# Vision tower with routed experts: patch matmuls on 128 filled rows, 21 pixels a group instead of 28, the rest moved by VectorE

## The reference

```python
patches = X.reshape(B, C, 8, 28, 8, 28).transpose(0, 2, 4, 1, 3, 5).reshape(B, 64, C * 28 * 28)
tokens = einsum('bpi,hi->bph', patches, W) + b            # 2352 inputs to 128 outputs
tokens = concatenate([cls, tokens], axis=1) * pos_embed
h = tokens
h = h + attention(layernorm(h), W_c)      # scores, softmax over a window of 64, sigmoid(concat @ W_c)
h = h + moe_ffn(layernorm(h), ...)        # norm, router, top 2 of 16 experts, shared expert, feed-forward
```

## Time and profile before

| | |
|---|---|
| median of three runs | 1130.94 us |
| the profiled execution | 1132.04 us, its span 1130.3 us |
| mean granted TensorE clock | 0.952 |
| TensorE busy | 1009.2 us, 89% |
| VectorE busy | 552.6 us, 49% |
| ScalarE busy | 640.3 us, 57% |
| GpSimd busy | 382.3 us, 34% |
| patch matmuls (line 1261) | 428.3 us, 896 records |
| pair copies (line 541) | 252.0 us, 224 of 1161 ns |

### The profile page before, as it was taken

The page is one execution under the profiler, slowest core; times in us unless marked ns, Lnnn a source line. Parts: engine busy times, 40 slices in busy tenths (PEclk is TensorE's granted clock), DMA queues, the critical chain, the costliest instruction groups (busy, mean ns, idle before and its releaser), DMA issues.

```text
span 1130.3 us, 20773 instructions
## 1 busy us (share of the span) xinstructions
PE 1009.2 (89%) x4911; PEld 665.4 (59%) x4911; DVE 552.6 (49%) x2019; ACT 640.3 (57%) x1056; POOL 382.3 (34%) x399
## 2 busy tenths in 40 slices
PE   3899999999999999999524899999999859898986
PEld 2344454555554454555314899999999635554554
DVE  3034544445445434445443666666666355555543
ACT  2566676666666776666213465556655426555554
POOL 0001222333333222333352122222222476666661
PEclk9899999999999999999656999999999979999999
DMA  9965566666656666661128688888888312222321
GB/s 228 236 172 148 169 180 182 183 183 204 186 178 178 173 180 181 188 189 37 38 86 269 201 249 249 247 247 249 248 244 237 102 53 80 79 80 80 87 60 35
DMA packets 208005, 186.36 MB, mean 165 GB/s; under 512 B 16909, under 2 KB 182378, under 8 KB 207722
## 3 DMA queue, kind: packets, MB, share of 16 engines
q1 hardware_dynamic: 192400, 156.82, 48.9%
q0 software_dynamic: 12256, 27.81, 7.4%
q10 hardware_dynamic: 3322, 1.44, 0.5%
HBM read 150.15 MB, written 35.85 MB: 165 GB/s over the span
## 4 chain that ended last, share of the span: by engine, by line
PE 71%; POOL 12%; issue 8%; SPq 3%; DVE 3%; DMA 2%; ACT 0%; DVEq 0%; POOLq 0%; ACTq 0%
PE bank L1261 36%; PE bank L1399 12%; PE bank L1388 10%; POOL region L799 9%; PE bank L1266 3%; SPq L376 2%; POOL rstd L733 2%; PE bank L1377 2%; PE bank L1274 1%; PE bank L1282 1%; PE bank L1296 1%; PE bank L1339 1%; PE bank L1341 1%; DVE region L881 1%; DMA region<-in_x 1%
## 5 line engine op out<-in xcount | busy, mean ns | idle before, releaser
L1261 PE MATMUL bank<-xf,wp 128*128 128x512 f32 x896 | 428.3, 618 | 7.6 <-ACT xf L541 7.6
L541 ACT ACTIVATE xf<-region 84x1024 f32<-84x1024 f32 x224 | 252.0, 1161 | 50.8 <-DMA region<-in_x 30.6
L1261 PEld LDWEIGHTS bank<-xf,wp 128*128 128x128 f32 x896 | 160.4, 190 | 182.2 <-issue 168.6
L647 ACT ACTIVATE region<-bank,cols 128x256 f32<-128x256 f32 x320 | 135.0, 477 | 119.1 <-PE bank L1388 119.1
L733 POOL TENSOR_TENSOR rstd<-var,neghalf 128x4 f32<-128x4 f32 (+2 forms) x51 | 63.1, 1237 | 390.4 <-DVE var L890 299.0
L1399 PE MATMUL bank<-region 128*128 128x128 f32 x1280 | 156.4, 276 | 0.0
L1399 PEld LDWEIGHTS bank<-region 128*128 128x128 f32 x1280 | 150.7, 193 | 0.0
L799 POOL DMA_INDIRECT region<-y_rows,gidx x130 | 126.4, 972 | 68.2 <-issue 36.3
L749 POOL DMA_INDIRECT z_rows<-z,posg x130 | 128.2, 986 | 37.5 <-issue 37.5
L1388 PE MATMUL bank<-parts 128*128 128x256 f32 x960 | 136.6, 292 | 3.8 <-DVE parts L1093 2.8
L778 POOL DMA_DIRECT2D y_rows<-region x80 | 58.1, 727 | 233.7 <-DVE region L1077 224.7
(11 more groups left out here) (169 smaller groups left out, 1123.8 us busy)
## 6 DMA issues: line engine op xcount, KB each, us to landing
region<-in_x SPq DMA_DIRECT2D x384, 196.0 KB
region<-in_L_ffn_ew SPq DMA_DIRECT2D x160, 256.0 KB, 3.4
region<-z_rows SPq DMA_DIRECT2D x80, 128.0 KB, 2.8
y_rows<-region POOLq DMA_DIRECT2D x80, 128.0 KB, 3.1
out<-region SPq DMA_DIRECT2D x65, 64.0 KB
ht_dram<-hT SPq DMA_DIRECT2D x16, 256.0 KB, 3.4
r_dram<-rr SPq DMA_DIRECT2D x16, 256.0 KB, 3.6
region<-ht_dram SPq DMA_DIRECT2D x16, 256.0 KB, 5.4
```

Source lines behind the costliest of these rows:

```text
L541: act.activation(pair_of(i)[0:KROWS], pixels(k, i), ACT.Copy).then_inc(xact_ready, 1)
L647: act.activation(ehT[n % 2][:, c], bank[1 + c][:, 0:EROWS], ACT.Silu, bias=bias[c])\
L1261: ins = pe.matmul(pa[:, :], wp[:, px], pair_of(i)[:, :, j], start=px == 0, stop=px == PATCH - 1)
```

## The change

A patch row of 28 pixels is split. The first 21 stay where they are and are the 21 steps of the matmul (`MAIN`). The last 7 (`EXTRA`) of every row are moved: rows 0 to 31, 32 to 63 and 64 to 83 (`BLOCKS`) each go as one block of 32, 32 or 20 partitions x 512 runs of 7 to partitions 96 and up, over the pixels 0 to 6, 7 to 13 and 14 to 20 there. So step s multiplies the 84 rows of pixel s and, in rows 96 to 127, a moved pixel; the weights are laid out the same way. The moves are made by VectorE, in place in `xb[k]`, between its other steps: block 0 of group g+2 before the gates of body g, block 1 at the end of body g, block 2 in body g+1 between `xh` and `h2`. The rows 84 to 95 and 116 to 127 of both buffers are zeroed once, by four DMAs of SyncE from a tile of zeros.

21 pixels are 10 pairs and an odd one, which has a buffer of its own (`xlast`). ScalarE copies all 128 rows and waits for the moves. `take_patch` now stands ahead of the first pair of group g+2. On TensorE the ranks of body g stand behind the last pair of group g+1.

```diff
-PAIRS = PATCH // 2
+MAIN = 21
+BLOCKS = ((0, 32), (32, 64), (64, KROWS))
+EXTRA = PATCH - MAIN
+W_TILES = -(-MAIN // 4)
+FOURTH = 96
+PAIRS = -(-MAIN // 2)
@@ buffers
-        wp = sb("wp", [P, PATCH, D])
+        wp = sb("wp", [P, MAIN, D])
+        xlast = sb("xlast", [P, GTOK])
@@ pixels and blocks
-            return xb[k][0:KROWS].rearrange("p (t x) -> p t x", x=PATCH)[:, :, 2 * i:2 * i + 2]
+            return xb[k].rearrange("p (t x) -> p t x", x=PATCH)[:, :, 2 * i:min(2 * i + 2, MAIN)]
+        def block_parts(k, n):
+            lo, hi = BLOCKS[n]
+            buf = xb[k].rearrange("p (t x) -> p t x", x=PATCH)
+            return buf[FOURTH:FOURTH + hi - lo, :, n * EXTRA:(n + 1) * EXTRA], buf[lo:hi, :, MAIN:PATCH]
@@ SyncE
+            def zero_gaps(k):
+                for lo, hi in ((KROWS, FOURTH), (FOURTH + BLOCKS[-1][1] - BLOCKS[-1][0], P)):
+                    n = zeros.shape[1]
+                    dst = xb[k][lo:hi].rearrange("p (r c) -> p r c", c=n)
+                    sp.dma_start(dst, zeros[lo:hi, :].unsqueeze(1).to_broadcast([hi - lo, XCOLS // n, n])).then_inc(gap_zeroed[k], 16)
             load_x(0, 0)
-            sp.wait_ge(wp_t, PATCH // 4)
+            sp.wait_ge(memset_done, 2)
+            zero_gaps(0)
+            sp.wait_ge(wp_t, W_TILES)
+            zero_gaps(1)
             load_x(1, 1)
@@ ScalarE
                 for i in range(lo, hi):
+                    for n in range(len(BLOCKS)):
+                        if 2 * i <= n * EXTRA < 2 * i + 2:
+                            act.wait_ge(block_moved, g * len(BLOCKS) + (n + 1))
+                    wait_slot(act, g, i)
+                    act.activation(pair_of(i)[:, :, 0:min(2, MAIN - 2 * i)], pixels(k, i), ACT.Copy).then_inc(xact_ready, 1)
...
-                high(4, 7)
+                high(4, 5)
                 take_x(g)
+                high(5, 7)
+                take_s(g)
                 high(7, 9)
-                take_s(g)
-                high(9, 10)
                 take_a(g)
-                high(10, 11)
+                high(9, PAIRS)
                 take_c(g)
                 take_z(g, k, h, nt)
-                high(11, 12)
                 take_r(g, k, h, nt)
                 route_b(g, nt)
-                high(12, 14)
-                high_next(0, 2)
                 if ahead:
                     take_patch(g + 1)
-                high_next(2, 3)
+                high_next(0, 1)
                 take_w(g + 1)
-                high_next(3, 4)
+                high_next(1, 4)
@@ VectorE, setup
-            for buf in (wp[64:P], xf[64:P]):
-                dve.memset(buf, 0.0).then_inc(pads_zeroed, 1)
+            dve.memset(wlaid, 0.0).then_inc(pads_zeroed, 1)
...
+            for j, (lo, hi) in enumerate(BLOCKS):
+                for c in range(CH):
+                    ...
+                    dve.tensor_copy(wlaid[:, at:at + CH * (rows - 1) + 1:CH, j * EXTRA:(j + 1) * EXTRA],
+                                    wnat[:, c, y:y + rows, MAIN:PATCH]).then_inc(w_laid, 1)
@@ VectorE, moves
+            def move_block(g, k, h, n):
+                if n == 0:
+                    if isinstance(g, int) and g < 2:
+                        dve.wait_ge(gap_zeroed[g], 32)
+                    dve.wait_ge(x_loaded[k], h * (16 * GIMG * CH) + 16 * GIMG * CH)
+                dst, src = block_parts(k, n)
+                dve.tensor_copy(dst, src).then_inc(block_moved, 1)
...
                     normalise(xh, h[k], mv, rstd1, GT).then_inc(xh_ready, 1)
-                low(5, 6)
+                move(2)
                 dve.wait_ge(t4_done, r + 1)
...
                 dve.tensor_scalar(rs2[:, 0:nt], rs2[:, 0:nt], -1.0, 0.5, ALU.mult, ALU.add).then_inc(rs_ready, 1)
-                low(8, 10)
+                move_next(0)
                 dve.wait_ge(l_done, r + 1)
...
                 dve.tensor_copy(posg[k][:, 0:nk], posf[:, 0:nk]).then_inc(pos_ready, 1)
-                low(13, 14)
-                if ahead > 1:
-                    copy_dve(r + 2, k, h_ + 1, 0, 3)
+                move_next(1)
@@ TensorE
-                    for j in range(2):
-                        px = 2 * i + j
-                        ins = pe.matmul(pa[:, :], wp[:, px], pair_of(i)[:, :, j], start=px == 0, stop=px == PATCH - 1)
+                    for s in range(2 * i, min(2 * i + 2, MAIN)):
+                        ins = pe.matmul(pa[:, :], wp[:, s], pair_of(i)[:, :, s % 2], start=s == 0, stop=s == MAIN - 1)
...
-                patches(9, 11)
+                patches(9, PAIRS)
                 ranks(g, nt)
-                patches(11, PAIRS)
```

## The result

The changed kernel takes **1136.53 us** (median; 1134.21 to 1141.36). The kernel before, on the same chip, takes 1131.76 us (1128.34 to 1133.21). The ratio is 1.005, with a 95% interval from 1.0032 to 1.0068: slower by half a per cent. The forecast was 1111 us in a range of 1098 to 1135, so the sign and the range are both missed. The profiled execution took 1137.45 us; its span is 1135.8 us.

What follows compares the result with a forecast made beforehand. TensorE, busy all 32.00 us of a stretch, bounds the kernel. After: 92 + 35.5 + 12 x 30.6 + 26.3 = 521.0 to the last body, against 541.9; 20.9 us off 1132.04 gives 1111 us, range 1098 to 1135.

Steps and rivals of the forecast that it cites:

- a zero fill, q: At the start, on SyncE's queue: each of four zero fills of 688 KB was taken at 4 us.
- second load landed: At the start: the second pixel load, queued behind the zero fills, was to land at 66 us.
- first load of the loop starts, E(1): End of the start: body 0's pixels are used and the loop's first load is issued, forecast at 92 us.
- from E(1) to the end of body 1: Into the loop: load landing 28.8 us, move 2.2, gates, ranks and W matmuls 4.47; 35.5 us together.
- a move, m: VectorE's copy of one block, three a group: 2.2 us, within bounds of 2.0 and 3.9.
- a round: One pass of the group loop: 30.0 us by the load's path, 30.6 with the clock loss, against 32.04 before.
- last body starts: End of the loop: the last body was to start at 521.0 us, against 541.9 before.
- The start: Section on the time before the loop: zero fills delay the second load, so the loop's first load starts at 92 us.
- The zero fills are slow: Rival, 30%: fills to 12 partitions hold up SyncE's queue; middle 1132.5 us, from 1126 to 1140.
- The clock's price: In the loop: TensorE's lower clock after idling ahead of the ranks costs 1.65 to 2.7 us each time.
- One element a cycle: Rival, 8%: VectorE's moves run at single rate, 3.9 us each, rounds of 32.6 us, 1135 us in all.
- filled rows: TensorE's matmuls: 128 filled rows cost no more; rival, 3%: they pull the clock to 0.9, giving 1130 us.

Runs made afterwards that it cites:

- e1: The kernel before, with only the change's four zero fills added at the same place in SyncE's queue: 1164.13 us, 1.0298 of before.
- e2: The kernel before, with 2.36 MB of zeros sent to all 128 partitions of idle buffers, same places in the queue: 1129.61 us, 0.9991 of before.
- e3: The changed kernel, with the empty rows zeroed by VectorE (first buffer) and GpSimd (second) instead of the four fills: 1103.29 us, 0.9757 of before.
- e9: The kernel before, with only the changed order (patch sum copied out ahead of the next pairs, ranks behind the last pair): 1131.4 us, 1.0005 of before.
- e10: The changed kernel with zeros by VectorE and GpSimd, and block 0's move right behind the ranks' operand, ahead of the other gates and positions: 1077.2 us, 0.9528.
- e6: The changed kernel with zeros by VectorE and GpSimd, and block 0's move behind the positions: 1093.41 us, 0.9675 of before.
- e16: The same kernel as e10, run again: 1077.49 us, 0.9527 of before.
- e17: e10 with six of the 24 transfers of each later load issued by GpSimd: 1081.44 us, 0.9561 of before.
- e4: The changed kernel, zero fills kept, with block 0's move placed behind the positions, beside block 1's: 1125.75 us, 0.9966 of before.
- e12: The kernel before, with one zero fill a buffer over 24 partitions (84 to 107), on a slower chip: 1230.6 us, 1.0114 of before.

## Why the prediction was wrong, step by step

| step | predicted | measured |
|---|---|---|
| a zero fill, q | 4 us | 8.5 us |
| second load landed | 66 us | 89.0 us |
| first load of the loop starts, E(1) | 92 us | 117.9 us |
| from E(1) to the end of body 1 | 35.5 us | 36.3 us (154.17) |
| a move, m | 2.2 us | 2.02 us |
| a round | 30.6 us | 30.39 us |
| last body starts | 521.0 us | 544.97 us |
| the time | 1111 us | 1136.5 us |

**The step that failed is the price of a fill, in "The start".** The text put it between 3 and 21 us and took 4, as if 12 of the 16 DMA engines shared a fill at the rate of the loads. It measured 8.5. Of the 25.9 us by which E(1) is late, four fills at 4.5 more are 18. Some 5 come between the fills' end and the landing of the load behind them: 50 us plus the fills' 34 are 84, and it was 89.0. The last 3 are body 0, from there to E(1): 28.9 us instead of 26, as its first records run slowly behind a wait of 19.47 us. The other 0.4 us of the 26.35 by which the profiled execution missed (1137.45 against 1111.1) are small terms: 0.8 more up to the end of body 1, 2.7 less in the rounds, 2.3 more behind the last body's start. e1, e2 and e3 show the cause from three sides.

**The rival had it.** "The zero fills are slow" was given 30%, and the estimate that it works out from the Trainium skill, "SBUF — State Buffer", "Door 1: The DMA port swizzle (why `[64,N]` ≈ `[32,N]`)", q = 8.4 us, is what was measured, to 0.1 us. The time by it, 1129 us, was still 7.5 short, since it left out the landing and body 0. For the same reason the gain was gone at 8.5 us a fill already, not only at 9.1 (by the text's own 20.9 us of gain over four fills it would have been 9.2). The choice of 4 was made against the only row that bore on it: 2.7 GB/s a partition, from 226 GB/s over 84 partitions, which would have given 21. Measured were 6.7 GB/s a partition (80 over 12). Neither end was near. The range's upper end, 1135, lay only 2.5 us above the rival's middle, 1132.5, though the text itself ran the rival up to 1140.

**The loop was right.** 28.8 us from E to landed were 28.9 (332.73 to 361.62). VectorE waited there as foretold, SyncE issued for 25.3 us, TensorE was released by m2. The idle time of 3.6 us a round came as 3 us in each round at first (3.16 at 151.21) and later as 7.56 in every second one, since SyncE's next load can't start sooner than 27.16 us after its last. The clock's price was put at 1.65 to 2.7 a time (the upper end of a round, 31.1, goes with the 2.9 of its row, 2.7 gives 31.0). Behind the wait of 7.56 us the W matmuls and t1 took 4.30 us (366.44 to 370.74) instead of 2.23, so 2.1. Behind the waits of 3 us in the first rounds the same piece cost between nothing (212.00 to 214.24) and 1.4 more (151.38 to 155.02). So the 30.39 that came close to 30.6 is a mean of rounds of 30.3 to 30.7 at first and of pairs of 27.2 and 34.4 later, which the text did not foresee.

**The move was right,** and the warning against it was not needed: 3584 words in runs of 7, with odd starts, went at 0.52 ns a word plus 0.16, as the earlier trace rows have it for runs of 28. The rule from the Trainium skill, "Vector Engine (DVE) Microarchitecture Reference", section 5.2, by which m would be an estimated 2.5, is not borne out by the 48 moves here (2.02 to 2.16 us; every source starts at word 21, and one destination of three at 7). The page's 1.30 ns is for a program with two sources, both at odd words; the moves have one. "One element a cycle" is out too.

**The order and the filled rows** cost or gave nothing: e9 shows it for the order, 623 ns a matmul record, against 618 before, for the rows. The setup's small edits were not run by themselves. The clock was 0.919 over the span, lower than before (0.952), but by TensorE's idling, not by its rows: from 332 to 364 us, between two waits, it is 1.00, and in e10, with short waits, 0.949 over the span.

**What the change could have given:** e3 is the change without its fills, 27 us under before. In the text's own terms, with the fills at nothing, it is no longer the second load that decides E(1) but group 0's pixels: read at 32.56, a move and a copy later 36.0, 21.8 long, 57.8; then 29.7 - 6.3 + 0.5 = 23.9 to E(1) = 81.7, which makes 1101 us. e3's 1103 lies 2 over that. Its E(1) is 83.6, and its first moves take 4 us longer beside GpSimd's zeros.

## What to carry to other kernels

A transfer's price depends on which partitions it touches, not only on its bytes: put a fill that touches a few partitions on an engine that idles, or spread it, and never queue it ahead of a load that starts the program. When matmuls are taken out, write down the next path (issue, landing, move, operand, matmul) with its own sum before counting the gain, and place an operation that waits for a load behind everything that another engine needs from the same engine: here that place was worth 26 us between e3 and e10, and one step too late (e6) gave only 10 of it.

## What the runs showed of the hardware

- Zeros copied inside SBUF, from and to the same partitions, went at 63 to 83 GB/s for partitions 84 to 95 and 116 to 127, at 154 GB/s for 84 to 107, and at some 145 for 84 to 127; with zeros for all 128 under way the DMA engines moved up to 367. The load queued behind the four narrow fills on SyncE landed at 89.0 us, and the fills took 34 us of that.
- VectorE's three moves took 6.13 us alone, and 9.71, 10.07, 10.17 and 13.69 us while GpSimd cleared a buffer (e10, e16, e3, e17). In e16 three moves and three memsets were each lengthened by 1.2 to 1.9 us; in e17 one move took 9.58 us, until GpSimd was through, and no memset was lengthened.
- TensorE's granted clock was 0.50 behind an idle time of 7.56 us. Behind 2.6 us its next pair took 2.07, 2.58, 3.05 or 3.52 us in different rounds of e4; behind 1.8 to 2.4 us in e10 it took 2.07, 2.62 or 3.19; behind 0.7 to 1.0 us always 2.07, where it takes 1.97 without a wait.
- On one chip the kernel before took 1223 us instead of 1130. In e12, which ran there, the patch matmuls were nearly as long (634 ns a record, 618 in the kernel before), but the rounds were 35.9 us (101.94 to 533.28), SyncE took 29.8 to 31.4 us to issue a load in most of them instead of 25.3, and ScalarE waited 54 us between 100 and 500 us for something outside the core's own engines, where the profile of the kernel before shows no such wait. What that is was not tried.
